# Three chunk buffers for the adjacency in place of two, in a two-layer graph kernel

## The reference

```python
def reference(x, adj, w1, w2, w3, bias, W, b, we1, be1, we2, be2):
    o = (adj == 1) @ (x @ w1) + (adj == 2) @ (x @ w2) + (adj == 3) @ (x @ w3) + bias
    x = layernorm(x + o)
    h = x @ W.T + b
    e = (h @ we1 + be1) + (h @ we2 + be2).T          # 8192 x 8192
    e = where(e >= 0, e, 0.01 * e)
    attention = softmax(where(adj > 0, e, -9e15), axis=1)
    return layernorm(x + attention @ h)
```

## Time and profile before

| | |
|---|---|
| time, median of 3 runs | 1710.22 us (1709.4 to 1712.68) |
| profiled execution | 1715.92 us, span 1714.3 us |
| mean granted TensorE clock | 0.946 |
| busy share: PE, DVE, ACT, POOL | 85%, 67%, 56%, 12% |
| adjacency loads (queue q0) | 67.12 MB, 128 issues, median 11.8 us to landing |
| all other transfers (queue q1) | 38.05 MB |

### The profile page before, as it was taken

One profiled execution on the slowest core, in us unless ns is written; L12 is line 12 of the kernel. 1 busy time (PEld: TensorE's weight loads), 2 busy tenths in 40 slices (PEclk: granted clock), 3 DMA queues, 4 the chain that ended last, 5 costly groups with the idle time before them and its releaser, 6 DMA issues. The chain is left out here.

```text
span 1714.3 us, 19415 instructions
## 1 busy us (share of the span) xinstructions
PE 1461.9 (85%) x6934; PEld 672.6 (39%) x6934; DVE 1140.8 (67%) x2384; ACT 959.5 (56%) x1454; POOL 206.0 (12%) x188
## 2 busy tenths in 40 slices
PE   3677787896997997997988589999999999999996
PEld 1323343342443443443434234444444444444443
DVE  4557767777697696786776576556566666666563
ACT  2223422633364445444434566777888787888774
POOL 1113213123122120121120220000000000000000
PEclk9889898898998998998998789999999999999998
DMA  9999889879788888788892210000001100000100
GB/s 117 120 125 98 93 83 108 93 73 106 86 86 100 74 93 100 73 92 94 76 106 34 62 37 7 25 1 25 26 25 40 35 25 25 25 25 25 32 1 14
DMA packets 122436, 106.46 MB, mean 62 GB/s; under 512 B 4768, under 2 KB 114912, under 8 KB 122336
## 3 DMA queue, kind: packets, MB, share of 16 engines
q0 software_dynamic: 67584, 67.12, 43.5%
q1 hardware_dynamic: 54752, 38.05, 7.8%
HBM read 294.39 MB, written 12.09 MB: 179 GB/s over the span
## 5 line engine op out<-in xcount | busy, mean ns | idle before, releaser
L960 ACT ACTIVATE neg_masks<-e_row,cols 128x512 int8<-128x512 f32 x1024 | 640.7, 708 | 214.4 <-PE ps L1156 149.3
L1156 PE MATMUL ps<-pos_masks,tables 128*128 128x512 fp8e4 x2048 | 623.4, 387 | 69.0 <-DVE pos_masks L589 64.3
L1156 PE MATMUL ps<-neg_masks,tables 128*128 128x512 fp8e4 x2048 | 621.1, 385 | 0.0
L1110 PE MATMUL ps<-edge_masks,tables 128*128 128x512 fp8e4 (+1 forms) x2048 | 475.9, 393 | 49.7 <-DVE edge_masks L568 34.1
L587 DVE TENSOR_TENSOR neg_masks<-pos_masks,neg_masks 128x2048 uint16<-128x2048 uint16 x128 | 158.5, 1238 | 281.5 <-ACT neg_masks L960 280.5
L1156 PEld LDWEIGHTS ps<-pos_masks,tables 128*128 128x128 f16 x2048 | 196.6, 99 | 325.8 <-issue 114.7
L1110 PEld LDWEIGHTS ps<-edge_masks,tables 128*128 128x128 f16 x2048 | 204.2, 101 | 306.2 <-DVE edge_masks L568 37.5
L1156 PEld LDWEIGHTS ps<-neg_masks,tables 128*128 128x128 f16 x2048 | 203.3, 99 | 251.7 <-issue 17.5
L568 DVE TENSOR_SCALAR edge_masks<-edges 128x512 uint16<-128x512 uint16 x512 | 110.4, 290 | 147.7 <-ACT edges L951 147.5
L945 ACT ACTIVATE packed_bf<-packed 128x1024 bf16<-128x1024 uint8 x64 | 67.4, 1053 | 250.4 <-DVE packed L558 250.4
L548 DVE TENSOR_TENSOR seen<-seen,adj_in 128x2048 uint16<-128x2048 uint16 x128 | 164.4, 1285 | 25.9 <-DMA adj_in<-adj 19.1
(11 more groups left out here) (115 smaller groups left out, 615.5 us busy)
## 6 DMA issues: line engine op xcount, KB each, us to landing
adj_in<-adj POOLq DMA_DIRECT2D x128, 512.0 KB, 11.8
e_row<-e_scratch SPq DMA_DIRECT2D x30, 256.0 KB, 4.2
edges<-x SPq DMA_DIRECT2D x8, 512.0 KB, 14.1
x_rows<-x SPq DMA_DIRECT2D x8, 512.0 KB, 5.4
x_scratch<-x SPq DMA_DIRECT2D x8, 512.0 KB, 9.1
edge_masks<-x_scratch SPq DMA_DIRECT2D x16, 256.0 KB, 3.2
out<-adj_in SPq DMA_DIRECT2D x16, 256.0 KB, 2.6
part_scratch<-a_c_rows SPq DMA_DIRECT2D x14, 256.0 KB, 5.0
```

The lines of the kernel that those rows point to most:

```text
L960: ins = e.activation(GN[:, n:n + GR].bitcast(I8), e1row[:, q % 2, :], ACT.Sign, bias=t2[:, JC * c + j:JC * c + j + 1])
L1110: ins = e.matmul(ps[:, h, :], v_hl[:, i, JC * c + j, :], U0[:, n:n + GR].bitcast(kind), start=c == 0 and j == 0 and i == 0, stop=c == NCH ...
L1156: ins = e.matmul(z_bank(q, k), tab[:, c, 2 * k + i, j, :], mask[:, n:n + GR].bitcast(F8A), start=first and j == 0 and i == 0, stop=final a ...
```

## The change

The tile `adj_in` holds three chunks of two halves in place of two chunks. A chunk k goes to buffer k modulo 3. GpSimd issues the loads of chunks 0, 1 and 2 before the loop, and in slot k the loads of chunk k+3, once chunk k has been packed. There is a pair of semaphores for each of the three buffers, and every wait on a landed chunk counts by three. The other users of `adj_in` keep their places at its start.

```diff
+NBUF = 3
-        in_raw = sb("adj_in", [P, 4 * 4 * CC], U8)
+        in_raw = sb("adj_in", [P, NBUF * 2 * 4 * CC], U8)
-        xr_b = in_raw[:, 3 * 4096:].bitcast(F32)...
+        xr_b = in_raw[:, 3 * 4096:4 * 4096].bitcast(F32)...
-        adj_row = in_raw[:, :].bitcast(BF16)
+        adj_row = in_raw[:, 0:2 * JB * P].bitcast(BF16)
         def half(k, h):
-            n = 4096 * (2 * (k % 2) + h)
+            n = 4096 * (2 * (k % NBUF) + h)
             return in_raw[:, n:n + 4096]
-        s_adj = [[sem(f"adj_in_{n}_{h}") for h in range(2)] for n in range(2)]
+        s_adj = [[sem(f"adj_in_{n}_{h}") for h in range(2)] for n in range(NBUF)]
         # SyncE, pieces of x
-                    e.wait_ge(s_adj[(v - 2) % 2][1], 16 * ((v - 2) // 2 + 1))
+                    e.wait_ge(s_adj[(v - 2) % NBUF][1], 16 * ((v - 2) // NBUF + 1))
         # GpSimd, load(k, h)
-                if k >= 2:
-                    e.wait_ge(s_seen, 2 * (k - 2) + h + 2)
+                if k >= NBUF:
+                    e.wait_ge(s_seen, 2 * (k - NBUF) + h + 2)
                     if h:
-                        e.wait_ge(s_p1, k - 1)
+                        e.wait_ge(s_p1, k - NBUF + 1)
                     else:
-                        e.wait_ge(s_pk, k - 1)
+                        e.wait_ge(s_pk, k - NBUF + 1)
...
-            for k in range(2):
+            for k in range(NBUF):
                 for h in range(2):
                     load(k, h)
...
             for k in range(K + 5):
                 for h in range(2):
-                    if 2 <= k + 2 < K:
-                        load(k + 2, h)
+                    if k + NBUF < K:
+                        load(k + NBUF, h)
         # VectorE, check_and_pack(k)
-                    e.wait_ge(s_adj[k % 2][h], 16 * (k // 2 + 1))
+                    e.wait_ge(s_adj[k % NBUF][h], 16 * (k // NBUF + 1))
```

More of the change, by code:

```diff
@@ L132, in build @@
         xr = [in_raw[:, 4096 * n:4096 * (n + 1)].bitcast(F32).rearrange("p (t d) -> p t d", d=D) for n in range(3)]
-        xr_b = in_raw[:, 3 * 4096:].bitcast(F32).rearrange("p (t d) -> p t d", d=D)
+        xr_b = in_raw[:, 3 * 4096:4 * 4096].bitcast(F32).rearrange("p (t d) -> p t d", d=D)
         num = in_raw[:, 0:4 * GT * (D + 1)].bitcast(F32).rearrange("p (t d) -> p t d", d=D + 1)
@@ L446, in load @@
                             adj[r:r + GR, c * CC:(c + 1) * CC].rearrange("(b p) c -> p b c", p=P))\
-                    .then_inc(s_adj[k % 2][h], 16)
-            for k in range(2):
+                    .then_inc(s_adj[k % NBUF][h], 16)
+            for k in range(NBUF):
                 for h in range(2):
```

## The result

The changed kernel takes 1716.64 us (median of 20 runs, 1712.65 to 1719.55) against 1710.21 us before (20 runs, 1705.54 to 1715.55). The ratio is 1.0037, 95% interval 1.0029 to 1.0045: 6.4 us slower. The forecast was 9.3 us slower. Its profiled execution took 1717.43 us; that of before was 5.7 us above the median of its own runs and this one 0.8 us above, so the two spans (1714.3 and 1715.7 us) understate the difference. I compare stretches of the two traces, not their ends.

What follows compares the result with a forecast made beforehand. The first 120 us were taken as set by x pieces sharing the DMA engines with adjacency loads. +10.3 us at piece 7 and -1.0 at the last load gave +9.3 on the 1710.22 median: 1719.5 us, range 1709.5 to 1725.

Steps and rivals of the forecast that it cites:

- No wait to remove: VectorE's adjacency waits at the start: a third buffer could remove at most 4.2 us, covered by ScalarE's wait for x.
- Nothing moves before 65 us: Start, through x piece 3 at 64.81 us: both kernels have an unbroken adjacency queue, so they are alike.
- The x pieces slow down beside a queue that never empties: x pieces after 65 us: each costs about 16.4 us while adjacency loads stay queued, against 13.2 us before.
- +10.3 us at piece 7: Last x piece lands at 127.8 us in place of 117.55, because the extra chunk keeps the adjacency queue full.
- lower bound from DMA work: x pieces from 65 to 117 us: extra chunk's 10.4 us of full engines less 4.2 us free share, leaving +6.2.
- Carried whole to the end: After piece 7: an earlier chunk earns nothing, so the x delay stays in full through the later slots.
- -1.0 us at the last load: Last superblock: chunk 63 loaded a slot earlier leaves the e1 row less traffic; bounds 0 and -2.5 us.
- Same: Rival, x loading: pieces keep their cadence and idle DMA room absorbs the extra chunk; 1710 to 1712 us; chance 0.24.
- faster: Rival, e1 rows in the first half: an empty queue saves 2.5 us each, 17.5 at most, 1702 us; chance 0.06.
- GpSimd was not blocked: Rival, first loads: a request ring too small for six blocks GpSimd; its result counted in the case of no change.

Runs made afterwards that it cites:

- third_from_slot8: Changed kernel with the third buffer filled only in slot 8, once all x pieces have landed: 1712.19 us, ratio 1.0001 against the kernel before.
- third_from_slot4: Changed kernel with the third buffer filled in slot 4, when x pieces 5, 6 and 7 are still to come: 1718.45 us, ratio 1.0044.
- second profile: Both kernels run and profiled again unchanged: changed kernel 1715.62 us, ratio 1.0023; kernel before 1711.52 us, ratio 1.0001.

## Why the prediction was right

- *No wait to remove.* Right, and more so than forecast: VectorE's waits are 18.8 us in place of 19.1, where I had given 15 to 17 as a sign. The two small ones, for the second halves of chunks 1 and 2, stayed. Chunk 2 was asked for at the start, yet its second half was there at 41.49 us, where it had been at 41.69: the transfers ahead of it are the same.
- *Nothing moves before 65 us.* Right within 1.1 us.
- *The x pieces slow down beside a queue that never empties.* Right in kind and, for pieces 4 to 6, in size: 15.9, 15.8, 17.1 against the 16.4 taken. The DMA share of 1.11 is the sign I had given (1.12), ScalarE's 65.8 us of waits for x are under the 70 of the forecast. third_from_slot8 takes the chunk away and the loss goes, third_from_slot4 asks for it later and the loss stays.
- *+10.3 us at piece 7.* This is the term that was too large: +5.9 measured (5.6 in the second profile). I had piece 7 at 127.8 us, in the middle between 125.2 and 130.4; it came at 123.44, before either. Of the 4.4 us between, 1.1 is piece 3, which came that much earlier, 0.3 is pieces 4 to 6, and 3.0 is piece 7 itself, 10.8 us in place of 13.8. The queue ran dry sooner than I had worked out: by the issues and landing times of line 446, chunk 6's first half landed at 81.8 us, not 82.7, and the seven gaps to the end of chunk 9 had a mean of 5.8 us, not 6.0. Chunk 9's halves in the changed kernel (issue times, us to landing):

```profile
L446 POOL DMA_DIRECT2D adj_in<-adj x2: 740/744/747, 106.3 to 107.0; - x2
DMA to landing us min/median/max: 10.4/13.0/15.7
```

  The second landed at 107.0 + 15.7 = 122.7 us, where I had 124.7, and piece 7 0.7 us after it, at the low end of the rule rather than in its middle. My lower bound from DMA work, +6.2, was the better estimate: an extra chunk of 10.4 us less the free room. The same sum fits third_from_slot4 (8.2 worked out afterwards, 8.3 measured).
- *Carried whole to the end.* Right from slot 9 to 61 (6.5 and 6.3 us in the first profiles), within the scatter: against the second profile of before it is 8.5 and 6.5 us. Between slots 7 and 9 the changed kernel gave back 2.6 us in its first profile and 1.2 in its second; the two profiles of before differ by 1.7 us over the same slots, so no cause is shown for it.
- *-1.0 us at the last load.* Not shown: the row scatters from 4.7 to 6.4 us within one kernel.
- *The rivals.* "Same" fell by a queue that stayed full; "faster" did not come from the change, but the price behind it was real and larger than I had put it: 4.4 to 4.9 us a superblock, in place of 2.5, once the traffic is really held. GpSimd was not blocked: its first six loads were issued from 1.4 to 5.4 us without a pause.

The trace agrees with the Trainium skill's rule of turns between queues ("DMA: Bandwidth & Descriptors", "Queues, rings and completion order") in that pieces take 15.8 to 17.1 us for as long as the other queue is not empty; the sum by it alone, 16.4 us for each piece, gave 130.4 us for piece 7 and was 7 us too high, because the queue did run dry before the last one.

## What to carry to other kernels

Before adding a buffer, find the wait that it would remove; here the reader of the buffer waited 19 us in 1714, all of it at the start. The deeper prefetch on shared DMA engines was not free: it moved bytes that nobody needed yet ahead of bytes that an engine was waiting for, and in the two cases measured here the price was close to its own transfer time less the idle room (6.2 worked out and 5.9 measured, 8.2 and 8.3). What paid in this kernel is the opposite, keeping the urgent transfers served: two requests in flight for x (about 9 us), and bulk loads held back while a row of 2 KB per partition is on the path (4.4 to 4.9 us each time, if the next row doesn't then queue behind them).

## What the runs showed that I had not expected

In this kernel a store of 4 KB takes 1.28 us from issue to the next request with no adjacency in flight and 4.1 to 5.6 us with it, and a row of 256 KB behind a backlog of four halves took 18.3 us where it takes 3.0 to 4.3 alone: the time of these transfers was set by what the adjacency loads had in flight. Asking for the x pieces two at a time changed their pace from 13.2 to 12.0 us with two buffers and from 15 to 12.0 with three, at the same bytes. And 2.0 us of the second half come or go from one execution to the next together with the granted clock of one stretch of 20 us.
